# A sparse expert stage with 79 block slots in place of 80, and its padding stores paired one to a load

## The reference, cut to what matters

```python
logits = jnp.einsum('th,eh->te', x, gate_w)
scores = jax.nn.softmax(logits, axis=-1)
topk_w, topk_idx = jax.lax.top_k(scores, K)                 # K = 2 of E = 16
combine = jnp.sum(jax.nn.one_hot(topk_idx, E, dtype=x.dtype) * topk_w[..., None], axis=1)
gu = jnp.einsum('th,ehj->etj', x, w_gate_up)                # 2 * 176 columns
h = _swiglu(gu, I)
y = jnp.einsum('eti,eih,te->th', h, w_down, combine)
```

## Time and profile before

| what | value |
|---|---|
| three runs: median (lowest to highest) | 1572.07 us (1571.59 to 1573.24) |
| the profiled execution's own time | 1568.67 us |
| its span, first to last instruction | 1566.6 us |
| mean granted TensorE clock | 0.985 |
| busy in the span: PE, DVE, ACT, POOL | 1461.3, 1216.8, 1007.9, 1018.6 us |
| last result copy of the expert stage starts | 1526.0 us into the span |

### The profile page before, as it was taken

How to read it: one execution, slowest core, us unless ns; L and a number is a source line. 1 busy time by engine, 2 the same in 40 slices (tenths; PEclk the granted TensorE clock), 3 DMA queues, 4 the chain that set the end, 5 groups by cost and what they waited for, 6 DMA issues and landing times.

```text
span 1566.6 us, 44812 instructions
## 1 busy us (share of the span) xinstructions
PE 1461.3 (93%) x16413; PEld 1082.4 (69%) x16414; DVE 1216.8 (78%) x2657; ACT 1007.9 (64%) x2399; POOL 1018.6 (65%) x1641
## 2 busy tenths in 40 slices
PE   9889999999899999998999999988999999899990
PEld 3557777776667777676677777766777777667870
DVE  6787788887777888886777778877777888676766
ACT  3666666666567666665666666666667666667770
POOL 4477764543788565666878787678877665286760
PEclk9999999999999999999999999999999999999995
DMA  7466933213464321334443333146342311348519
GB/s 206 75 130 152 178 75 72 52 25 70 84 121 82 63 53 36 65 62 86 81 95 56 62 68 60 39 72 119 69 74 61 66 31 30 97 135 261 154 52 324
DMA packets 331076, 144.66 MB, mean 92 GB/s; under 512 B 278546, under 2 KB 321589, under 8 KB 330872
## 3 DMA queue, kind: packets, MB, share of 16 engines
q1 hardware_dynamic: 305296, 104.57, 33.5%
q10 hardware_dynamic: 18664, 20.52, 4.6%
q0 software_dynamic: 6912, 16.83, 3.4%
HBM read 47.04 MB, written 29.53 MB: 49 GB/s over the span
## 4 chain that ended last, share of the span: by engine, by line
PE 69%; DVE 9%; DMA 5%; ACT 5%; issue 4%; POOL 3%; SPq 2%; POOLq 0%; DVEq 0%; ACTq 0%
PE of_ps L783 28%; PE s_ps L783 25%; PE t_ps L980 14%; DMA qT<-work 3%; DVE pT L1840 1%; ACT work L1194 1%; ACT probs L1316 1%; DVE smax L1813 1%; DVE weights L2059 1%; ACT pT L1191 1%; PE of_ps L1105 1%; PE t_ps L1091 1%; DMA work<-y_exp 1%; ACT probs L1321 1%; DVE work L1637 1%
## 5 line engine op out<-in xcount | busy, mean ns | idle before, releaser
L1840 DVE TENSOR_TENSOR pT<-t_ps,pT 128x512 f16<-128x512 f32 (+3 forms) x688 | 410.7, 597 | 130.5 <-ACT pT L1191 127.4
L1191 ACT CAST pT<-t_ps 128x512 f16<-128x512 f32 (+3 forms) x688 | 355.1, 516 | 229.5 <-PE t_ps L980 228.6
L783 PE MATMUL s_ps<-kT,qT 128*128 128x512 f16 (+3 forms) x2112 | 473.2, 336 | 5.1 <-DMA qT<-work 5.1
L980 PE MATMUL t_ps<-id,probs 128*128 128x128 f32 x2304 | 378.9, 279 | 12.8 <-DVE pT L1840 6.4
L980 PEld LDWEIGHTS t_ps<-id,probs 128*128 128x128 f32 x2304 | 257.2, 141 | 95.3 <-issue 45.4
L783 PEld LDWEIGHTS of_ps<-ckv,pT 128*128 128x128 f16 x6912 | 241.8, 98 | 40.1 <-DVE o_sb L1669 8.4
L783 PE MATMUL of_ps<-ckv,pT 128*128 128x64 f16 x6912 | 258.6, 193 | 5.7 <-DVE o_sb L1669 5.4
L783 PEld LDWEIGHTS s_ps<-kT,qT 128*128 128x128 f16 x2112 | 202.9, 98 | 73.9 <-DMA qT<-work 6.1
L1316 ACT ACTIVATE probs<-s_ps,nmax 128x640 f32<-128x640 f32 (+3 forms) x256 | 245.7, 960 | 0.1
L783 PE MATMUL of_ps<-weights,xT 128*128 128x128 f16 (+1 forms) x930 | 197.4, 348 | 17.8 <-DVE work L1637 8.2
L1802 DVE TENSOR_REDUCE nmax<-s_ps 128x1 f32<-128x640 f32 (+3 forms) x200 | 192.3, 962 | 18.3 <-PE s_ps L783 18.0
(11 more groups left out here) (248 smaller groups left out, 2396.0 us busy)
## 6 DMA issues: line engine op xcount, KB each, us to landing
wgu_sb<-wgu ACTq DMA_DIRECT2D x8, 704.0 KB, 5.5
work<-lists SPq DMA_DIRECT2D x40, 128.5 KB, 2.5
qT<-lists SPq DMA_DIRECT2D x40, 128.5 KB, 2.3
x<-x SPq DMA_DIRECT2D x32, 128.0 KB, 2.6
dense<-den SPq DMA_DIRECT2D x32, 128.0 KB
weights<-dense ACTq DMA_DIRECT2D x1, 4096.0 KB, 24.2
qT<-y_exp SPq DMA_DIRECT2D x16, 256.0 KB, 6.6
work<-y_exp SPq DMA_DIRECT2D x16, 256.0 KB, 8.2
```

Of the source, the lines that this page charges most:

```text
L783: return pe_.matmul(o, a, b, start=start, stop=stop)
L980: last = pe_.transpose(t_ps[:, h, c * P:(c + 1) * P], probs[:, u % 2, g * L + j * P:g * L + (j + 1) * P], id32[:, :])
L1191: return act.copy(o, i)
L1840: dve.tensor_tensor(pT[:, u % 2, 1, h, 0:w], t_ps[:, h, 0:w], pT[:, u % 2, 0, h, 0:w], ALU.subtract).then_inc(s.lo_p, 1)
```

## The change

`FULL` stays at 64 and `NMT` becomes 79. The rows number exactly 64 times 128. If all 64 full slots are used, there are no partial blocks at all; otherwise at most 63 are, and slot 63 is free. So slot 63 now holds the last full block or, failing one, the partial block of expert 15, and slots 64 to 78 hold the partial blocks of experts 0 to 14. The table's last instruction takes the smaller of the block's row and `rest_row` (the partial block of expert 15) in slot 63, and of the block's row and `DUMMY` in the other slots (`not_last` is 0 in slot 63's partition and `DUMMY` in the others). The three small columns that this needs lie in `amax_e`. SP's loads of slots 32 to 78 are written out instead of looped; a pad follows each of the loads 32 to 47, and the wait for all pads stands ahead of load 63.

```diff
-NMT = (NT * P * TOPK) // P + E
+FULL = (NT * P * TOPK) // P
+NMT = FULL + E - 1
...
-        base_p = sb("base_p", [P, 1], F32)
+        base_p, rest_row, not_last = (amax_e[:, k:k + 1] for k in range(3))
...
-            with sp.Fori(EARLY // XG, EARLY // XG + PAD_ROUNDS) as m:
-                for q in range(XG):
-                    later_rows(m, q)
-                    if q % 2:
-                        write_pad((m - EARLY // XG) * (E // PAD_ROUNDS) + q // 2)
-            sp.wait_ge(s.pads, 16 * (E + 1))
-            with sp.Fori(EARLY // XG + PAD_ROUNDS, NMT // XG) as m:
-                for q in range(XG):
-                    later_rows(m, q)
+            for e in range(E):
+                later_rows(EARLY // XG, e)
+                write_pad(e)
+            for n in range(EARLY + E, NMT):
+                if n == FULL - 1:
+                    sp.wait_ge(s.pads, 16 * (E + 1))
+                later_rows(n // XG, n % XG)
             for q in range(XB):
-                sp.wait_ge(m_out[q], 16 * (NMT // XB))
+                sp.wait_ge(m_out[q], 16 * len(range(q, NMT, XB)))
...
-            for e in range(E):
+            for e in range(E - 1):
                 n = FULL + e
                 h_transposes(n, n % 2)
-                if e + 2 < E:
+                if n + 2 < NMT:
                     expert_up(n + 2, n % 2, e + 2)
-                if e + 4 < E:
+                if n + 4 < NMT:
                     xg_transposes(n + 4, (n + 4) % XG, n % 2, (n + 4) // XG)
                 expert_down(n, n % 2, e)
...
-            with act.Fori(EARLY // XB, NMT // XB - 1) as m:
+            with act.Fori(EARLY // XB, ROUNDS - 1) as m:
                 for q in range(XB):
                     expert_round(m, q, m * XB + q)
-            for q in range(XB):
-                expert_round(NMT // XB - 1, q, NMT - XB + q)
+            for n in range((ROUNDS - 1) * XB, NMT):
+                expert_round(ROUNDS - 1, n % XB, n)
...
             def later_blocks():
                 link(dve.tensor_reduce(tiles_e[:, :], cmp_k[:, :, :], AX_X, ALU.add))
-                dve.scalar_tensor_tensor(tab[0:1, 0, FULL:NMT], tiles_e[0:1, :], float(P), first_e[0:1, :], ALU.mult, ALU.add)
-                dve.tensor_copy(tab[0:1, 1, FULL:NMT], iota_e_sb[0:1, :])
+                dve.scalar_tensor_tensor(tab[0:1, 0, FULL:NMT], tiles_e[0:1, 0:E - 1], float(P), first_e[0:1, 0:E - 1], ALU.mult, ALU.add)
+                dve.tensor_copy(tab[0:1, 1, FULL:NMT], iota_e_sb[0:1, 0:E - 1])
+                dve.scalar_tensor_tensor(rest_row, tiles_e[:, E - 1:E], float(P), first_e[:, E - 1:E], ALU.mult, ALU.add)
                 link(dve.tensor_tensor(left_e[:, :], tiles_e[:, :], taken[:, :], ALU.subtract))

             def later_jumps():
+                dve.tensor_scalar(not_last, iota_p_sb[:, 0:1], float(FULL - 1 - EARLY), float(DUMMY), ALU.not_equal, ALU.mult)
                 link(dve.tensor_tensor_scan(ends[:, :], ones_e[:, :], left_e[:, :], 0.0, ALU.mult, ALU.add))
...
-                link(dve.tensor_scalar(t_row, t_row, float(DUMMY), None, ALU.min))
+                link(dve.scalar_tensor_tensor(t_row, rest_row, not_last, t_row, ALU.max, ALU.min))
...
-            with dve.Fori(EARLY // XB, NMT // XB - 1) as m:
+            with dve.Fori(EARLY // XB, ROUNDS - 1) as m:
                 for q in range(XB):
                     tile(m * XB + q, q % 2)
-            for n in range(NMT - XB, NMT):
+            for n in range((ROUNDS - 1) * XB, NMT):
                 tile(n, n % 2)
```

More of the change, by code:

```diff
@@ L53 @@
 EARLY = 32
-FULL = NMT - E
 XG = 16
-PAD_ROUNDS = 2
 LN_STEPS = 14
@@ L353, in build @@
         XB = YB = 8
+        ROUNDS = -(-NMT // XB)
         def carve(view, at, shape, dt):
```

## The result

The change made the kernel slower. The median of ten runs is 1578.59 us (1574.39 to 1584.08), against 1573.09 (1568.19 to 1575.77) for ten runs of the kernel before; the ratio is 1.0036, with a 95% interval of 1.0023 to 1.0048. That is 5.5 us more where 1.9 less were forecast, outside the range and on the side to which 5% were given. The profiled execution took 1578.55 us, its span is 1576.7. It is a typical one of its kernel; the profiled execution before, 1568.67, lies at the low end of its own ten, so part of the 10 us between the two spans is scatter. I compare stretches, not spans.

A forecast was written before the change was run, and what follows sets the result against it. TensorE's own work was taken to bound the expert stage, and the DMA engines the 37 us behind it. -2.00 for the slot and +0.1 for DVE gave -1.9, from 1572.07 to 1570.2 us, range 1568.0 to 1572.5.

The forecast's parts named there:

- the side to which 5% were given: Whole kernel slower by over 0.2%, resting on SP falling too far behind: chance 0.05.
- A slot less: Expert stage: one slot's 20 matmuls leave TensorE's unbroken chain, everything at the end starts one slot earlier: -2.00 us.
- the distance of 2.00 unchanged: Sign for the expert stage: slots stay 2.00 us apart on TensorE after the change.
- The rule and the row: SP's table reads: skill's 600 ns floor would make the sum about +4.8 us; set aside for the trace's 272 ns median.
- The table on DVE: Behind slots 16 to 18: two added instructions and one of changed kind cost +0.1 us (0.07 to 0.34).
- Pads and loads: SP's loads 32 to 47 with pads: pairs of 2.4 us, 8.4 us of cover at slot 47, so nothing.
- The first rival: SP's pairs too slow, TensorE waits at slot 47's transposes; at 3.4 us a pair the median is 1576.8: chance 0.05.
- Contention: Crowded stretch 1410 to 1434: more pad traffic, 7% or 0.15 us, counted as nothing; bounds nothing and 2.2 us.
- The second and third rival: Crowded stretch 1410 to 1434: traffic stretches it again, up to 2.2 us, chance 0.08; or gives 2.2 us back, chance 0.05.
- Behind the stage, unchanged: After the expert stage: the DMA-bound 37 us stay as before, with 2.30 us for the last landing.
- The sum: Whole kernel: -2.00 + 0.1 = -1.9 us, from 1572.07 to 1570.2 us.

The follow-up runs named there:

- h3: The changed kernel with plain copies (h2), table rows kept at 80 entries, 79 used: 1559.91 us, 1.86 under h1 and 7.9 under h2.
- m3: h3 once more (79 slots, table rows of 80 entries), against the control repeated on one chip: 1561.96 us against 1563.51, 1.55 less.
- h4: h1 with table rows of 81 entries, so the second row starts at 324 bytes; 80 slots stay: 1570.0 us, 8.23 over h1.
- h2: The changed kernel with plain copies for the attention part's transposing DMAs, against h1: 1567.82 us, 6.05 over.
- m1: The control (kernel before, plain copies) with each read of four experts split into two reads of two registers: 1571.32 us, 2.6 under the kernel before.
- k4: h1 with SP's part of the change alone (written-out loads, paired pads, moved wait): 1557.65 us, 11.1 under the kernel before; k2 beside it 1557.19.
- k2: h1 with table rows of 84 entries, second row at 336 bytes: 1557.19 us, 11.5 under the kernel before.
- k3: h1 with the read of four experts split into four reads of one register: 1575.51 us, 6.8 over the kernel before, 18.3 over k2.
- k1: h1 with table rows of 82 entries, second row at 328 bytes: 1566.6 us, 2.1 under the kernel before, 9.4 over k2.
- h1: The control: the kernel before with the attention part's transposing DMAs replaced by plain copies of the same bytes: 1561.77 us.

## Why the prediction was wrong, step by step

- **"A slot less", -2.00 us: right in size as far as h3 and m3 show it, wrong as the whole of it.** This is the step that failed. It took for granted that the slots that stay keep their price (the sign was "the distance of 2.00 unchanged") and put any change to them at nothing, without a reason: it counted only the instructions that run, and these are the same. `NMT` is also the width of a table, and the diff doesn't show that line, since it reads `NMT` before and after. The term for the moved row, +8.2 us by h4, was missing: TensorE's 17 reads took 1.07 us each in place of 0.33, and -1.9 became +6 (h2; +5.5 in the changed kernel). None of the rivals had it, and the 5% for "slower" stood on SP.
- **What the profile could have told.** The 17 reads on line 1124 stand in the same answer as the row on SP's reads the earlier trace rows, at 332 ns for four entries beside 272 for one. I took SP's row and left theirs out. That the edit moved their address was to be seen in the declaration. What a moved address costs, no row of the kernel before shows; but that it moved was reason enough for a rival.
- **The rule and the row.** The Trainium skill's 600 ns as the floor of a register load (DMA: Bandwidth & Descriptors, section on latency and other measured facts) is not borne out here: SP's reads stayed at 269 ns in the median. (By the prediction's own working that case comes to +4.7 us, where it wrote +4.8.) But I used a row on reads of one entry to dismiss a rule on reads in general, and the reads of four entries on the other engine went over that figure. The Trainium skill has a nearer sentence (Runtime: NRT & Kernel Launch, section on instruction fetch mechanics): register loads cost about 200 ns per register even in bulk, said there of loads from HBM. Here, from SBUF, m1 shows 0.235 us for the second register, which is near it, and the aligned read of four at 0.33 us is outside it.
- **The table on DVE, +0.1 us: right in size.** The added instruction behind slot 16 starts 0.07 us ahead of the next one, and the product follows as before, 0.19 us after it. Behind slot 18 the product follows the changed instruction after 0.36 us, 0.29 before, a little more than the 0.02 to 0.06 said. What `not_last` costs behind slot 17 was not singled out.

```profile
1402.87 0.14 DVE L1927 SCALAR_TENSOR_TENSOR amax_e<-tiles_e,first_e 128x1 f32<-128x1 f32 x1
1402.94 0.15 DVE L1928 TENSOR_TENSOR left_e<-tiles_e,taken 128x16 f32<-128x16 f32 x1
1403.13 0.34 DVE L1978 SCALAR_TENSOR_TENSOR work<-work,s_ps 128x176 f32<-128x176 f32 x1
...
1408.61 0.21 DVE L1939 SCALAR_TENSOR_TENSOR t_tab<-amax_e,t_tab 128x1 f32<-128x1 f32 x1
1408.97 0.34 DVE L1978 SCALAR_TENSOR_TENSOR work<-work,s_ps 128x176 f32<-128x176 f32 x1
```

- **Pads and loads, nothing: right.** Pairs of 2.48 us on average in k4 (2.4 said) and 7.0 us of cover at slot 47 (8.4 said). The first rival, SP too far behind, is out. In the changed kernel load 32, which "should not move", went out at 1411.45 in place of 1407.20: it waits for the results of slot 16, and these were late. The loads were still in time, since TensorE was later yet: load 47 at 1449.23 (1441 to 1448 said) for transposes at 1463.30, 14.1 us ahead.

```profile
1449.23 0.34 SPq L627 DMA_DIRECT2D qT<-lists  x1
```

- **Contention, nothing: right as far as seen.** k4 has all pads in half the slots and takes 172.1 us from the first to the last result copy, as k2 does with the old order. The second and third rival are out by the same two rows, one trace each.
- **Behind the stage, unchanged: right.** 37 us at a DMA share of 0.95, and 2.25 us for the last landing, 2.30 before.
- **The sum without the missing term** is -1.9 us; h3 and m3 have -1.86 and -1.55, with the interval of -3.5 to -0.2 that is given above.

## What to carry to other kernels

When a constant changes, look for every declaration that uses it, since a smaller table can move what lies behind its first row. Give each row of a table that TensorE's queue reads into registers a start at a multiple of 16 bytes and read four entries at a time; pad the row rather than cut it. (Reads of several entries on another engine's queue weren't tried.) When a changed kernel shows "issue" gaps in front of an engine that waits for nobody, compare the durations of its queue's register reads before and after: they are in no busy time.

## What the runs showed of the hardware that I had not expected

- A read of registers from SBUF on TensorE's queue takes 0.30 us for one entry (k3), 0.54 for two (m1) and 1.04 to 1.07 in the median for four that start at a multiple of 4 or 8 bytes alone (h4, k1), but 0.33 for four that start at a multiple of 16 bytes (h1, k2).
- TensorE's queue runs far enough ahead to cover a read of 0.33 us in every fourth slot completely (16.00 of 16.00 us busy in h1), and not one of 1.04 us (15.68 in h4).
- The same kernel before had medians of 1568.72, 1573.71 and 1573.95 us on three chips, a spread larger than the slot in question is worth. Differences of 2 us needed a control on the same chip.
